# Cross-attention: another placement of the score maxima, a softmax chain that starts a tile earlier, and two of its steps on GpSimd instead of VectorE

## The reference

```python
q = (x @ w_q).reshape(b, n, 16, 64)
kv = (context @ w_kv).reshape(b, m, 2, 16, 64)       # m = 1601
attn = softmax(einsum('bnhd,bmhd->bhnm', q, k) * 64 ** -0.5)
out = einsum('bhnm,bmhd->bnhd', attn, v).reshape(b, n, 1024)
return out @ w_out + b_out
```

## Time and profile before

| what | value |
|---|---|
| median of three runs | 2050.54 us (2050.0 to 2052.01) |
| the profiled execution, its own time | 2053.94 us |
| its span, first to last instruction | 2052.2 us |
| TensorE busy | 1746.8 us, 85% |
| VectorE busy | 1191.0 us, 58% |
| ScalarE busy | 832.0 us, 41% |
| GpSimd busy | 1323.0 us, 64% |
| mean granted TensorE clock | 0.919 |

### The profile page before, as it was taken

How to read it: one execution, slowest core, us unless ns; L and a number is a source line. 1 busy time by engine, 2 the same in 40 slices (tenths; PEclk the granted TensorE clock), 3 DMA queues, 4 the chain that set the end, 5 groups by cost and what they waited for, 6 DMA issues and landing times. The chain is left out here.

```text
span 2052.2 us, 32755 instructions
## 1 busy us (share of the span) xinstructions
PE 1746.8 (85%) x10682; PEld 1212.3 (59%) x10682; DVE 1191.0 (58%) x2046; ACT 832.0 (41%) x1228; POOL 1323.0 (64%) x711
## 2 busy tenths in 40 slices
PE   7553599999989999998999999899999998509990
PEld 5443466666656666665666666566666664408980
DVE  4788555556565656556565665655565654553345
ACT  3111234444444444444444444444444444224440
POOL 2988338577676667576776676675766677454544
PEclk8775689999999999999999999999999999559995
DMA  5000200000200000010000001000000000321223
GB/s 185 1 21 24 79 1 22 1 22 0 73 1 22 22 3 22 0 52 22 21 1 23 1 21 52 21 22 1 21 1 21 15 1 1 124 84 63 71 63 128
DMA packets 37813, 68.09 MB, mean 33 GB/s; under 512 B 3560, under 2 KB 27504, under 8 KB 36656
## 3 DMA queue, kind: packets, MB, share of 16 engines
q1 hardware_dynamic: 33936, 56.12, 8.1%
q0 software_dynamic: 3744, 10.23, 1.5%
HBM read 52.84 MB, written 13.50 MB: 32 GB/s over the span
## 5 line engine op out<-in xcount | busy, mean ns | idle before, releaser
L1001 POOL TENSOR_TENSOR xa_total<-xa_total,xa_pexp 128x1024 f32<-128x1024 f32 (+1 forms) x352 | 852.9, 2423 | 52.7 <-ACT xa_pexp L942 27.3
L1060 DVE TENSOR_REDUCE xa_parts<-ps_ring 128x1 f32<-128x402 f32 x1024 | 532.3, 565 | 299.8 <-PE ps_ring L887 292.8
L942 ACT ACTIVATE xa_pexp<-ps_s 128x1024 f32<-128x1024 f32 (+1 forms) x416 | 422.7, 1025 | 419.0 <-PE ps_s L842 391.9
L856 PE MATMUL ps_pv<-xa_pexp,xa_v 128*64 128x512 f32 (+1 forms) x1664 | 399.8, 604 | 0.0
L887 PE MATMUL ps_ring<-xa_k_hi,xa_q_hi 64*128 64x402 f32 x1024 | 235.0, 377 | 32.7 <-DVE xa_parts L1060 31.4
L856 PEld LDWEIGHTS ps_pv<-xa_pexp,xa_v 128*64 128x64 f32 (+1 forms) x1664 | 106.2, 137 | 181.9 <-issue 148.3
L887 PEld LDWEIGHTS ps_ring<-xa_k_hi,xa_q_hi 64*128 64x128 f32 x1024 | 142.7, 186 | 118.2 <-DVE xa_parts L1060 58.9
L1001 POOL TENSOR_TENSOR xa_total<-xa_pexp 128x1024 f32<-128x1024 f32 x32 | 76.3, 2384 | 190.9 <-ACT xa_pexp L942 189.6
L1048 DVE TENSOR_TENSOR xa_k_lo<-ps_ring,xa_k_hi 128x402 fp32r<-128x402 f32 (+1 forms) x128 | 73.6, 575 | 214.7 <-ACT xa_k_hi L953 214.7
L842 PE MATMUL ps_s<-xa_q_hi,xa_k_hi 64*128 64x512 f32 (+1 forms) x832 | 194.0, 433 | 3.6 <-DVE xa_k_lo L1048 2.8
L842 PE MATMUL ps_s<-xa_q_neg,xa_row_one 64*128 64x512 f32 (+1 forms) x832 | 174.4, 393 | 0.0
(11 more groups left out here) (263 smaller groups left out, 2946.2 us busy)
## 6 DMA issues: line engine op xcount, KB each, us to landing
wa_raw<-in_pack_a SPq DMA_DIRECT2D x17, 768.0 KB, 4.4
ex_w_raw<-in_pack_e SPq DMA_DIRECT2D x8, 1026.0 KB, 5.3
ctx_raw<-in_ctxT SPq DMA_DIRECT2D x4, 1601.0 KB, 8.5
wb_raw<-in_pack_b SPq DMA_DIRECT2D x16, 256.0 KB, 2.6
ex_w_hi<-ybuf SPq DMA_DIRECT2D x8, 512.0 KB, 7.6
sa_xT<-in_xT SPq DMA_DIRECT2D x8, 256.0 KB, 6.4
X<-in_x SPq DMA_DIRECT2D x1, 2048.0 KB, 11.5
x_hi<-sa_x1s_hi SPq DMA_DIRECT2D x16, 128.0 KB, 2.1
```

The lines of the kernel that those rows point to most:

```text
L856: ins = nc.tensor.matmul(ps_pv[half(h), :], v[0:m, t, at:at + XD], pexp[0:m, buf, h, :], start=t == 0, stop=t == MT - 1)
L942: nc.scalar.activation(pexp[0:m, buf], ps_s[0:m, (p * MT + t) % 2], ACT.Exp, scale=XD ** -0.5)\
L1001: nc.gpsimd.tensor_tensor(total[p][0:m], first, pexp[0:m, buf], ALU.add).then_inc(s["add_done"], 1)
L1060: nc.vector.tensor_reduce(parts[:, h, q, c:c + 1], ps_ring[:, r, 0:CW], AX.X, ALU.max)\
```

## The change

The tables of maxima change: a group also behind tile 0, second groups ahead of tiles 2, 10 and 12 instead of 4, 7, 10 and 12 (16 groups as before). The four reciprocals come at tiles 3, 4, 5 and 6 instead of 4, 5, 6 and 7, R2 at tile 6 instead of 7, R3 at 7 instead of 8; R4 stays at 8 and the OPs at 9. R2 and R4 are executed by GpSimd instead of VectorE, with the same waits. The closing chain behind the last block is in the same order as before, with R2 and R4 on GpSimd too.

```diff
-MX_BEFORE = (0, 0, 0, 0, 1, 0, 0, 1, 0, 0, 1, 0, 1)
-MX_BEHIND = (0, 1, 1, 1, 1, 1, 1, 1, 1, 1, 1, 1, 1)
+MX_BEFORE = (0, 0, 1, 0, 0, 0, 0, 0, 0, 0, 1, 0, 1)
+MX_BEHIND = (1, 1, 1, 1, 1, 1, 1, 1, 1, 1, 1, 1, 1)
...
-    return {3: ([("RS", p)], []), 4: ([], [("R1", p, 0)]), 5: ([], [("R1", p, 1)]), 6: ([], [("R1", p, 2)]),
-            7: ([], [("R1", p, 3), ("R2", p)]), 8: ([], [("R3", p), ("R4", p)]),
+    return {3: ([("RS", p)], [("R1", p, 0)]), 4: ([], [("R1", p, 1)]), 5: ([], [("R1", p, 2)]),
+            6: ([], [("R1", p, 3), ("R2", p)]), 7: ([], [("R3", p)]), 8: ([], [("R4", p)]),
             9: ([], [("OP", p, 0, back), ("OP", p, 1, back)])}
...
                 if kind == "PV" and st[2] >= 1:
                     add(pool, n, st)
+                elif kind == "R2":
+                    pool.wait_ge(s["inv_ready"], n.of("R1"))
+                    pool.wait_ge(s["pv_copied"], n.of("R2") + 1)
+                    need(pool, s["att_ready"], n.of("R4"))
+                    nc.gpsimd.tensor_tensor(att[:], pv_sb[:], inv[:], ALU.mult).then_inc(s["att_done"], 1)
+                elif kind == "R4":
+                    pool.wait_ge(s["att_hi_done"], n.of("R4") + 1)
+                    nc.gpsimd.tensor_tensor(att_lo[:], att[:], att_hi[:].bitcast(F32), ALU.subtract)\
+                        .then_inc(s["att_ready"], 1)
...
-                elif kind == "R2":
-                    dve.wait_ge(s["inv_ready"], n.of("R1"))
-                    dve.wait_ge(s["pv_copied"], n.of("R2") + 1)
-                    need(dve, s["att_ready"], n.of("R4"))
-                    nc.vector.tensor_tensor(att[:], pv_sb[:], inv[:], ALU.mult).then_inc(s["att_done"], 1)
-                elif kind == "R4":
-                    dve.wait_ge(s["att_hi_done"], n.of("R4") + 1)
-                    nc.vector.tensor_tensor(att_lo[:], att[:], att_hi[:].bitcast(F32), ALU.subtract)\
-                        .then_inc(s["att_ready"], 1)
```

## The result

| what | before | after |
|---|---|---|
| median, runs side by side | 2051.4 us (20 runs) | 2047.75 us (20 runs) |
| ratio of the times | | 0.9984, 95% interval 0.9977 to 0.9991 |
| the profiled execution, its own time | 2053.94 us | 2049.99 us |
| its span | 2052.2 us | 2048.3 us |
| TensorE, VectorE, GpSimd busy | 1746.8, 1191.0, 1323.0 us | 1746.2, 1102.8, 1391.8 us |

What follows compares the result with a forecast made beforehand. TensorE was taken to bound the kernel, busy 458.67 of 480 us in the steady stretch. Terms -11.6 + 7.9 - 5.1 + 3.2 + 0.4 = -5.2, plus 11.9 for the clock, gave +6.7: median 2057.2 us, range 2040 to 2069.

Steps and rivals of the forecast that it cites:

- TensorE sets the time, and its stalls at tiles 6, 7 and 9 go: Steady stretch: TensorE busy 458.67 of 480 us; 1.77 us saved at tiles 6 and 7, 0.96 at tile 9 (p = 0).
- A new stall at tiles 2 and 3, RS 0.95 us later: Ahead of RS, five groups of maxima instead of three; RS 0.95 us later, of which 0.38 is moved work.
- Blocks p = 1, -0.77 each: Fifteen blocks p = 1 with maxima: OP ready 0.77 us earlier, no wait for R4, -11.6 us in all.
- R2 and R4 at 1.24 us on GpSimd: On GpSimd each of the two takes 1.24 us, bounds 1.21 and 1.27; the skill's rule would give 1.4.
- The gap of 2.4 us ahead of OP in the twelve blocks p = 0, +0.66 each: Regular blocks p = 0: TensorE waits 2.4 us for R4 at tile 9, OP 0.66 us later, +7.9 us in all.
- The clock, 7 of 12 x 1.7 = +11.9: Behind the gaps in blocks p = 0 the clock falls in 7 of 12, 1.7 us each; bounds 0 and +20.4.
- Sequence ends, -1.7 each: Three sequence ends: OP starts near 955.6 instead of 957.26 us, -5.1 in all; bounds nothing and -3.5 each.
- First block, +0.4: The first block has the new stall and had not the old one: +0.4 us.
- Last block and chain, +3.2: Last round: R2 and R4 on GpSimd cost +2.1 us in the last block, +1.1 in the closing chain.
- The forecast's own range: The main forecast, clock falls in about half the blocks or somewhat more: 2051 to 2063 us, chance 0.5.
- Rival 1: TensorE waits 2.4 us at tile 9 but the clock holds: -5.2, 2045.3 us; needs three falls or fewer; chance 0.25.
- Rival 3: R4 is not late in blocks p = 0, so no wait or clock loss: -34.7, 2015.8 us; chance 0.05.

Runs made afterwards that it cites:

- experiment 1: The changed kernel with R2 and R4 back on VectorE, so only the new tables and chain against the kernel before: 2030.17 us, ratio 0.9892.
- experiment 2: The changed kernel with the old tables and old chain, so only R2 and R4 moved to GpSimd against the kernel before: 2028.74 us, ratio 0.9892.
- Experiments 3 and 4: The changed kernel with R3 and R4 ahead of the PVs of tile 7 (2012.88 us); the changed kernel with R4 alone back on VectorE (2019.82 us).
- experiment 3: The changed kernel with R3 and R4 ahead of the PVs of tile 7, so ahead of the two adds: 2012.88 us, ratio 0.9797.
- the executions with six falls: The changed kernel run twice more, unedited, to see how often the clock falls: 2046.65 and 2046.09 us.

## Why the prediction missed its sign

The path was right: the old ring stalls go, and R4 behind two adds makes a new gap. Two terms of the sum failed in size. The gain of the blocks p = 1 was put at 0.77 us each and measured 1.22, and a fall of the clock was put at 1.7 us and measured 1.1 to 1.3. Step by step:

- **TensorE sets the time, and its stalls at tiles 6, 7 and 9 go.** Right: 31.4 us of ring waits became 1.9.
- **A new stall at tiles 2 and 3, RS 0.95 us later.** Right at RS: in the block p = 1 that begins at 678.13 us, RS comes 14.42 us after the `negmax` row, before 13.47. The next step failed: "everything up to the scores of tile 6 stays 0.93 (p = 0) to 0.99 (p = 1) late". The PV of tile 5 is only 0.74 late (21.19 against 20.45): the PV directly ahead of the scores does not eat up the 0.19 us of the group that no longer stands ahead of tile 4, as I had it. The PV of tile 7 comes 1.03 us earlier, not 0.77.
- **Blocks p = 1, -0.77 each.** Too small; -1.22 measured (-18.3 / 15), and this is the largest error, 6.7 us. 0.26 is the point above. Another 0.2 lies between the PV of tile 9 and the OPs, 3.39 us against 3.58; the schedule makes it, since experiment 1 has 3.41 there, but by which wait was not looked for. Of the 1.22, 0.3 needs the move to GpSimd as well: with R2 and R4 on VectorE and the new schedule (experiment 1) the blocks give 0.92 each, because the PVs of tiles 7 and 9 lie 6.19 us apart, against 5.89 in the changed kernel.
- **R2 and R4 at 1.24 us on GpSimd.** Right: 1.27 and 1.26. The Trainium skill, GPSIMD Engine Reference, section 4.1 (Engine selection), whose rule speaks against this move, would have each at about twice VectorE's 0.69. The measured ratio is 1.8, and it holds only for an undisturbed VectorE. Beside GpSimd's adds VectorE took 0.8 to 2.6 us for R2 (before, and experiment 1); the last section shows what sets it. The same page, section 1 (Specifications), says that the two engines share their SBUF interfaces and contend when VectorE reads two inputs from there; the rows agree, since R2 grew while the maxima, with one input and that from PSUM, did not, and experiment 2 shows the move as a gain.
- **The gap of 2.4 us ahead of OP in the twelve blocks p = 0, +0.66 each.** Right: 2.24 to 2.36 us, and ordinary blocks without a fall are 0.61 us longer. Experiments 3 and 4 show the cause to be the adds ahead of R4.
- **The clock, 7 of 12 x 1.7 = +11.9.** The number of falls was near (10, 6, 6), the price was not. The prediction took lost clock for lost time: behind 480.77 the rows give (1 - 0.57) x 4 = 1.7 us of clock, as forecast, but from the OP to the PV of tile 11 the block needs 5.79 us where one without a fall needs 4.74, 1.05 more. Without a fall, that stretch is not bound by the clock alone. With six falls the term is some 7 us, 5 less than forecast.
- **Two blocks at the start of a pass of the outer loop.** Not foreseen. They cost +1.7 us each without a fall, 1.1 more than ordinary ones. Every kernel with the new tables has such blocks 2.4 to 2.6 us longer than its next block p = 0 (without a fall), the two with the old tables 1.4 to 1.5, so it comes with the tables. The group that now stands behind tile 0 is the likely reason, though no run moves it alone. In the changed kernel VectorE is idle on instruction issue ahead of the first maxima, and TensorE stops behind it:

```profile
1112.51 2.03 DVE L1069 TENSOR_REDUCE xa_parts<-ps_ring 128x1 f32<-128x402 f32 x4 [3.05 <-issue]
```

```profile
1113.14 0.44 PE L887 MATMUL ps_ring<-xa_k_hi,xa_q_hi 64*128 64x402 f32 x1 [0.86 <-DVE xa_parts L1069]
```

- **Sequence ends, -1.7 each.** Right in size (-1.9 to -2.0), by luck, for the mechanism was another: "holds GpSimd until about 954.2" put the delay into the adds; it is R4 that meets VectorE's split and takes 2.85 us:

```profile
944.92 3.42 DVE L1049 TENSOR_TENSOR xa_ctx_lo<-ctx_raw,xa_ctx_hi 128x1601 fp32r<-128x1601 f32 x1 [1.86 <-ACT xa_ctx_hi L984]
946.61 2.85 POOL L1016 TENSOR_TENSOR xa_att_lo<-xa_att,xa_att_hi 128x512 fp32r<-128x512 f32 x1
```

- **First block, +0.4.** Wrong, -0.2. It had no old stall by my reading, and the new one costs it nothing.
- **Last block and chain, +3.2.** Right in kind, +2.3 to +2.5.

Against the executions with six falls (-4.7 and -5.1 by their blocks) the forecast was 11.4 and 11.8 us too high: some 6.7 in the blocks p = 1, 5 in the clock and 2 in the last three points together, less 2.2 for the blocks at the loop's start. The medians put it at 10.3. The forecast's own range, 2051 to 2063, missed the measured 2047.75 by 3 us; the stated range, 2040 to 2069, holds it. Rival 1, "the clock holds", came nearest with 2045.3, and that was luck: its condition was three falls or fewer, and there were 6 to 10. Its rule that four falls decide the sign failed with the price of a fall and the blocks p = 1. Rival 3, "R4 is not late", had 5% and 2015.8 us: it was wrong for this change, but its price is near that of the version one line away, 2012.9 us.

## What to carry to other kernels

When a step moves to an in-order engine, list what stands in that queue between the step's last input and its consumer, and put the step ahead of the work that nobody is waiting for; here two adds of 2.4 us, due only later, cost 35 us of a gain of 39 us (experiment 3). Run both halves of a change alone: two halves that each give 1.1% and together give 0.2% name a collision. And price a fall of the clock from equal blocks with and without it, not from the granted clock times the stretch.

## What the runs showed of the hardware

The same idle gap in the same code is followed by half clock in one execution and not in another: 2.33 us at the same block, 0.66 and then 1.00. Gaps of 4.6 us at the sequence ends were followed by 0.50 in every one of nine cases. Gaps of 2.8 us in experiment 2 were followed by 1.00 twice and by 0.58 once. Behind the gaps of 1.0 us of experiment 1 the next 4 us were at 1.00.

The 128x512 product R2 took VectorE 2.60 us beside GpSimd's adds and GpSimd 1.27 us while VectorE reduced maxima, so the slower engine was twice as fast in place; when VectorE ran its own two-input instruction on the context, GpSimd's 1.26 us became 2.85 us.

These long times are waits, not slower work. In the kernel before, VectorE's R2 or R4, each with two inputs in SBUF, began 50 times while an add ran on GpSimd. All 50 ended 0.55 or 0.56 us behind the end of that add, however much of it was left, so that they took 0.80 to 2.83 us: in the earlier trace rows R2 ends at 765.97, in the earlier trace rows the add at 765.42. It holds the other way round: R2 or R4 on GpSimd began 15 times during VectorE's split, in five traces, and ended 1.12 us behind it each time, as in the two rows of the sequence end above (949.46 and 948.34). So of two such instructions the later one waited until the earlier was through, and its time is what was left of the other plus a fixed part. The maxima, read from PSUM, took 0.51 to 0.58 us each, beside adds and without them.
